# u and B loaded as 64 zero-padded rows on a new pitch in a Mamba scan on one core

## The reference

```
normed = rmsnorm(xn); x_z, z = split(normed @ in_proj_W)
xc = silu(conv4(x_z) + conv_b); dt = clip(softplus(xc @ dt_W + dt_b), 0.001, 0.1)
Bp = xc @ B_W; Cp = xc @ C_W; A = -exp(A_log)
for t in 0..511:
    h = exp(dt_t * A) * h + dt_t * B_t * x_t      # h is (8, 256, 64)
    y_t = sum_n h * C_t
x1 = xn + (y * silu(z)) @ out_proj_W; x1 + gated MLP(rmsnorm(x1)); + binary MLP(xn)
```

## Time and profile before

| | |
|---|---|
| runs | 1114.2, 1123.52, 1129.43 us |
| profiled execution, its own time | 1115.98 us |
| its span, first to last instruction | 1114.2 us |
| mean granted TensorE clock | 0.960 |
| PE, DVE, ACT, POOL busy | 87%, 84%, 82%, 76% of the span |
| HBM read, written | 303.24 MB, 22.02 MB |

### The profile page before, as it was taken

One profiled execution on the slowest core, in us unless ns is written; L12 is line 12 of the kernel. 1 busy time (PEld: TensorE's weight loads), 2 busy tenths in 40 slices (PEclk: granted clock), 3 DMA queues, 4 the chain that ended last, 5 costly groups with the idle time before them and its releaser, 6 DMA issues.

```text
span 1114.2 us, 27718 instructions
## 1 busy us (share of the span) xinstructions
PE 967.9 (87%) x8006; PEld 426.6 (38%) x8006; DVE 935.2 (84%) x2131; ACT 908.7 (82%) x1093; POOL 847.9 (76%) x1216
## 2 busy tenths in 40 slices
PE   5998883668999999998999887899998899999897
PEld 3555540113333343433333332334343334343436
DVE  5677663799989999997998887899998899999983
ACT  1666776789999999997988887899997899998980
POOL 6555513789888889887888786898887788988880
PEclk9999996789999999999999999899999899999999
DMA  4234358999999999997999999799999799999940
GB/s 139 81 136 180 136 200 298 345 327 355 351 343 334 345 355 350 345 344 268 356 341 332 319 328 318 271 351 352 353 349 333 280 366 343 339 356 340 335 148 10
DMA packets 76758, 327.39 MB, mean 294 GB/s; under 512 B 13472, under 2 KB 32800, under 8 KB 41504
## 3 DMA queue, kind: packets, MB, share of 16 engines
q1 hardware_dynamic: 76576, 325.30, 83.6%
HBM read 303.24 MB, written 22.02 MB: 292 GB/s over the span
## 4 chain that ended last, share of the span: by engine, by line
DVE 27%; PE 25%; POOL 19%; issue 16%; DMA 5%; ACT 5%; SPq 2%; DVEq 1%; POOLq 0%; ACTq 0%
POOL decayed L593 13%; DVE ps L1221 9%; PE ps L798 8%; DVE state L1232 7%; PE ps L743 5%; PE ps L897 5%; DMA decay<-dt_stage 4%; PE ps L883 3%; DVE h L1336 2%; ACT state L1030 2%; DVE h L1345 1%; DVE soft L1147 1%; POOL soft L543 1%; SPq L392 1%; POOL u_rest L553 1%
## 5 line engine op out<-in xcount | busy, mean ns | idle before, releaser
L593 POOL TENSOR_TENSOR decayed<-decay,state 128x256 f32<-128x256 f32 x1024 | 725.5, 733 | 169.1 <-DVE state L1232 125.4
L1010 ACT ACTIVATE decay<-decay,a_col 128x2048 f32<-128x2048 f32 x256 | 512.7, 2003 | 46.3 <-DMA decay<-dt_stage 36.5
L1232 DVE TENSOR_TENSOR state<-decayed,ps 128x256 f32<-128x256 f32 x1024 | 403.1, 417 | 55.4 <-POOL decayed L593 40.0
L1221 DVE TENSOR_TENSOR ps<-decay,ps 128x512 f32<-128x512 f32 x512 | 352.6, 689 | 40.5 <-ACT state L1030 17.2
L1030 ACT COPY state<-ps 128x512 f32<-128x512 f32 x512 | 288.9, 582 | 64.6 <-issue 43.2
L798 PE MATMUL ps<-state,c_cols 128*32 128x256 f32 x4096 | 338.2, 403 | 0.1
L743 PE MATMUL ps<-moving,b_rows 64*128 64x256 bf16 x1024 | 204.3, 281 | 100.5 <-DVE ps L1221 96.3
L750 PE MATMUL ps<-moving,b_rows 64*128 64x256 bf16 x1024 | 205.4, 282 | 12.0 <-DMA b_rows<-b_stage 12.0
L883 PE MATMUL ps<-h,w 128*128 128x256 f32 x512 | 175.8, 429 | 1.0 <-DVE h L1336 0.8
L743 PEld LDWEIGHTS ps<-moving,b_rows 64*128 64x128 bf16 x1024 | 58.4, 94 | 274.0 <-DVE ps L1221 172.3
L798 PEld LDWEIGHTS ps<-state,c_cols 128*32 128x32 f32 x4096 | 82.0, 109 | 113.4 <-issue 101.3
(11 more groups left out here) (124 smaller groups left out, 825.3 us busy)
## 6 DMA issues: line engine op xcount, KB each, us to landing
decay<-dt_stage SPq DMA_DIRECT2D x512, 512.0 KB, 6.6
moving<-u_stage SPq DMA_DIRECT2D x64, 288.0 KB
b_stage<-b_parts SPq DMA_DIRECT2D x24, 384.0 KB, 3.8
b_rows<-b_stage SPq DMA_DIRECT2D x64, 144.0 KB
dt_stage<-dt_tok SPq DMA_DIRECT2D x8, 512.0 KB, 3.1
u_stage<-u_parts SPq DMA_DIRECT2D x8, 512.0 KB, 2.8
x_tok<-in_L_attn_x_dram SPq DMA_DIRECT2D x4, 512.0 KB, 3.5
u_stage<-u_parts SPq DMA_DIRECT2D x8, 256.0 KB, 2.1
```

What stands on the lines that cost most here:

```text
L593: nc.gpsimd.tensor_tensor(decayed[:, p], decay[:, dec_slot(m, k), p, k % TS, :], state[:, (k - 1) % RING, p * E:(p + 1) * E], ALU.mult).th ...
L1010: nc.scalar.activation(pair, pair, ACT.Exp, scale=a_col[:, 2:3]).then_inc(decay_ready, 1)
L1221: nc.vector.tensor_tensor(ps[:, acc_bank(m, k), :].rearrange("p (q e) -> p q e", q=HQ), decay[:, dec_slot(m, k), HQ:Q, k % TS, :], ps[:, a ...
L1232: nc.vector.tensor_tensor(state[:, k % RING, p * E:(p + 1) * E], decayed[:, p], ps[:, SELFP + k % 2, p * E:(p + 1) * E], ALU.add).then_inc ...
```

## The change

- The 3 x 3 pairs of parts become 4 x 4 (NS = NP + 1): a fourth part of u and of B, and its pairs, are zeros. A load of u or B thus has 4 * 4 * 4 = 64 rows and they go to every second partition (`slice(hq, P, HQ)`), so that the two hq cover all 128 partitions of `moving`.
- The rows of the stages are T + TC = 528 tokens long instead of 512: 264 KB for u and 132 KB for B. `dt_stage` has one more row group of 8 KB for each bb.
- SP stores the zero parts at the beginning, 3 * B = 24 transfers (`store_pads`), from a corner of `moving` that POOL sets to zero first; SP waits for all of them before the first load of the scan.
- The two memsets of `moving` (L578 on POOL, L1202 on DVE) are gone.

```diff
+    TROW = T + TC
-    ROWS = NP * NP * HALF
-    RSTEP = 3
-    RFIRST = HROW + RSTEP - 1 - RSTEP * (ROWS // 2)
+    NS = NP + 1
+    ROWS = NS * NS * HALF
+    assert HQ * ROWS == P
...
-    u_stage = nc.dram_tensor("u_stage", (HQ, HQ, 2, NP, T, E), BF16, kind="Internal").ap()
-    dt_stage = nc.dram_tensor("dt_stage", (2, T // TS, Q, TS, E), F32, kind="Internal").ap()
-    b_stage = nc.dram_tensor("b_stage", (HQ, HQ, 2, NP, NP, T, 2 * N), BF16, kind="Internal").ap()
+    u_stage = nc.dram_tensor("u_stage", (HQ, HQ, 2, NS, TROW, E), BF16, kind="Internal").ap()
+    dt_stage = nc.dram_tensor("dt_stage", (2, T // TS + 1, Q, TS, E), F32, kind="Internal").ap()
+    b_stage = nc.dram_tensor("b_stage", (HQ, HQ, 2, NS, NS, TROW, 2 * N), BF16, kind="Internal").ap()
...
         def product_rows(hq):
-            first = RFIRST - 2 + hq
-            return slice(first, first + RSTEP * (ROWS - 1) + 1, RSTEP)
+            return slice(hq, P, HQ)
...
                          u_stage[hq, :, :, :, bass.ds(t, TC), :].rearrange("f b i t e -> (f b i) (t e)")
-                         .unsqueeze(1).broadcast_to([HALF * NP, NP, TC * E])
+                         .unsqueeze(1).broadcast_to([HALF * NS, NS, TC * E])
...
+                def store_pads(n):
+                    q, bb = n // 2, n % 2
+                    u_rows, b_planes = u_stage[q % HQ, q // HQ, bb], b_stage[q % HQ, q // HQ, bb]
+                    zeros = moving[:, 1, 0:2 * NS].rearrange("p t e -> p (t e)")
+                    sp.dma_start(u_rows[NP, 0:T].rearrange("(p j) e -> p (j e)", j=NJ),
+                                 zeros[:, 0:NJ * E]).then_inc(pads_stored, 16)
+                    sp.dma_start(b_planes[NP, :, 0:T].rearrange("k (p j) n -> p k (j n)", j=NJ),
+                                 zeros[:, 0:NS * NJ * 2 * N].rearrange("p (k n) -> p k n", k=NS)).then_inc(pads_stored, 16)
+                    sp.dma_start(b_planes[0:NP, NP, 0:T].rearrange("k (p j) n -> p k (j n)", j=NJ),
+                                 zeros[:, 0:NP * NJ * 2 * N].rearrange("p (k n) -> p k n", k=NP)).then_inc(pads_stored, 16)
...
+                sp.wait_ge(pad_zeroed, 1)
+                for n in range(B):
+                    store_pads(n)
                 for q in range(Q):
...
                 sp.wait_ge(rows_zeroed, 2)
+                sp.wait_ge(pads_stored, 16 * PADS)
...
                 nc.gpsimd.memset(zero_b[:], 0.0)
+                nc.gpsimd.memset(moving[:, 1, 0:2 * NS], 0.0).then_inc(pad_zeroed, 1)
...
-                    nc.gpsimd.memset(moving[:, 0], 0.0)
                     nc.gpsimd.memset(b_rows[:, 0], 0.0).then_inc(rows_zeroed, 1)
...
-                    nc.vector.memset(moving[:, 1], 0.0)
                     nc.vector.memset(b_rows[:, 1], 0.0).then_inc(rows_zeroed, 1)
```

More of the change, by code:

```diff
@@ L46, in mamba_and_binary_mlp_block @@
     HROW = P // 2
-    ROWS = NP * NP * HALF
-    RSTEP = 3
-    RFIRST = HROW + RSTEP - 1 - RSTEP * (ROWS // 2)
-    assert RFIRST > 0 and HROW + HQ - 1 + RSTEP * (ROWS // 2) <= P
+    NS = NP + 1
+    ROWS = NS * NS * HALF
+    assert HQ * ROWS == P
     QE = Q * E
@@ L118, in mamba_and_binary_mlp_block @@
         b_loaded = [sem("b_loaded0"), sem("b_loaded1")]
+        pad_zeroed = sem("pad_zeroed")
         rows_zeroed = sem("rows_zeroed")
+        pads_stored = sem("pads_stored")
         const_set = sem("const_set")
@@ L212, in mamba_and_binary_mlp_block @@
         STORES = 2 + NP
+        PADS = 3 * B
         def batches(eng, slot, filling=None):
@@ L400, in store @@
                     wait_all(sp, [(S["dt_ready"], n + 1)])
-                    sp.dma_start(dt_stage[bb, :, q].rearrange("(p c) s e -> p c (s e)", s=TS, p=P),
+                    sp.dma_start(dt_stage[bb, 0:T // TS, q].rearrange("(p c) s e -> p c (s e)", s=TS, p=P),
                                  dt_tok[:, bb].rearrange("p (c s) e -> p c (s e)", s=TS)
@@ L416, in store @@
                         wait_all(sp, [(S[ready], n + 1)])
-                        sp.dma_start(stage[i0:i1].rearrange("i (p j) e -> p i (j e)", j=NJ),
+                        sp.dma_start(stage[i0:i1, 0:T].rearrange("i (p j) e -> p i (j e)", j=NJ),
                                      parts[:, bb, i0:i1].rearrange("p i j e -> p i (j e)")
                                      ).then_inc(S[f"parts_stored{bb}"], 16)
+                sp.wait_ge(pad_zeroed, 1)
+                for n in range(B):
+                    store_pads(n)
                 for q in range(Q):
```

## The result

The changed kernel took 1180.29 us (median of four runs, 1177.52 to 1183.88) against 1120.83 us before in the same comparison. The ratio is 1.058, 95% interval 1.0534 to 1.0626: 5.8% slower. The forecast was 1112 us with a range up to 1170.

The account below looks back on a forecast made before the run. The compute chain was taken to bound a clean body at 54 us, DMA just under it. Span 1114.2 - 6 - 1 - 1 = 1106 us, 1108 us with 1.8 us around it; forecast median 1112 us, range 1090 to 1170 us.

Parts of the forecast that it names:

- The bound: Scan body: the compute chain sets a clean body at 54 us, with DMA just under the point where it takes over.
- Loss by slow packets: Scan loads of u and B: slow stretches cost 4.8 us of DMA per body, taken as removed by the change.
- The sum: Scan body if the loss grows with bytes: 50.1 + 8.5 = 58.6 us of DMA against 54 us compute, +74 us.
- The rival: Scan becomes DMA-bound: slow packets stay and grow with the 64 distinct rows, 1155 to 1190 us; chance 0.2.
- Memsets: Before the scan: DVE and POOL lose their memsets of `moving`; -1 us (0 to -2.1).
- Pads: Preparation: SP issues 24 pad stores in about 12 us, in a gap, done by some 53 us; cost 0.
- Start of the scan: First two chunks' loads: faster packets against more zeros, including PE's 12.3 us wait; together -1 us (-3 to +3).
- The rate with fast packets: Scan body afterwards: 403 GB/s as full rate, an ordinary body at 373 GB/s or so, still 54 us.

## Why the prediction was wrong, point by point

- **The bound** was read rightly. DMA stood just under the compute chain: the run with an eighth of u and B shows the floor at 1101 us, about 20 us below the kernel before in the same comparison. I had only 9.4 us for the loop from two long bodies of one execution, plus the start.
- **The failed step is "Loss by slow packets ... I take 'removed'".** I named three things that set load_u and load_b apart (pitch, destination rows, number of engines), saw that the change took all three away, and let the loss of 4.8 us per body go. Instead the bodies became 4.1 us longer on average. None of the three was the cause by itself: not the pitch (nothing clear of the noise in four pairs of runs), not the destination rows (the changed kernel has those of the dt loads and is slow), not the number of engines (48 rows are slow on 16). What I did not list is the form of the source against the destination. The load of u kept a source of two dimensions, 12 x 3 before and 16 x 4 afterwards, and it can be read in the diff: `.unsqueeze(1).broadcast_to(...)`. For B the change did what I expected, once u no longer slowed it: it is fast with u from one row and B untouched (1102 us, landing after 6.8 us). Against the changed kernel this cause is shown. That the kernel before was slow for its form as well (36 rows, u with one step or as 12 x 3) is shown only in so far as its data, addresses and partition step are ruled out.
- **The sum** with the loss growing was in the text: 58.6 us of DMA per body, +4.6 us over the chain, +74 us in all. Measured +4.1 us per body on average and +66.6 us on the span (the ordinary body shown, +7.2, is one of the long ones). The rival's 1155 to 1190 us held 1180. Its mechanism, many distinct rows, is refuted: 64 distinct rows are fast and 36 equal ones slow. Its arithmetic (the loss goes with the bytes of the slow loads, from a point at which the slack is used up) came out near, in part by luck: it leaves out what the bodies show beyond DMA times. A late dt load holds ACT, ACT holds the slots, and DMA then idles (the slices of 121 and 158 GB/s), and PE's granted clock falls behind such a wait; in other bodies the chain covers the loss.
- **What the Trainium skill said.** Page "DMA: Bandwidth & Descriptors", section "Latency and other measured facts": next to nothing lost at 512 KiB, and so nothing to win by padding 256 and 128 KB. That was my inference from the skill's figures, and the runs agree with it: 0.06 to 0.4% between the medians of the two pitches in the four pairs, no more than their intervals allow for. I had it in the rival to which I gave 0.2. The Trainium skill's rule for the number of engines (same page, section "Why a DMA increments its semaphore by 16 and not by 1") agrees with the completions in both traces. It does not follow that 16 are faster.
- **Memsets** -1 us: the scan begins 1.4 us earlier. That is the change's: the first load_u is at 173.3 to 174.7 us in the seven runs with the memsets and unchanged stores, at 171.6 to 173.2 us in the seven without. **Pads** 0: right in effect, though the issues took twice as long, 25.9 us instead of 12. One took SP up to 1.3 us, once 2.4, instead of 0.5, while DMA was busy throughout. The last is issued at 38.16 us, the load of x for n = 4 only behind it, at 39.02 us instead of the 25 that I had, and the store of n = 0 at 40.40 instead of 39.39 us, which nobody waited for. **Start of the scan**: PE's wait 13.5 us instead of 12.3, within the range given but on the other side of my -1 us.
- **The rate with fast packets** was right, though not of the changed kernel: with 64 single rows an ordinary body takes 54 us at some 375 GB/s and DMA is off the path.

## What to carry to other kernels

When a load makes its neighbours slow, list every respect in which it differs from a fast one, the dimensions of both access patterns included, and change them one at a time before paying bytes for all of them together. Zeros that round a transfer up are worth it only if they bring it into the fast form; here 78% more bytes of u and B cost nothing with 64 rows against 64 (0.4 to 0.5% below the kernel before) and 5.8% without. Read the rate in short slices against the best slice, since the busy share is at 9 tenths either way.

## What the runs showed of the hardware that I had not expected

- A load from DRAM of 64 rows to every second partition runs at full rate beside others when its source is 64 rows with one step, or one row 64 times. A source of 16 x 4 for the same 64 rows, 48 rows against 48 on 16 engines, and 36 rows on 12 engines do not: dt loads land in 6.6 to 9.3 us (median) instead of 5.9 to 6.1, and the rate falls to between 200 and 290 GB/s instead of some 400 for microseconds.
- As far as tried, this does not depend on the addresses: equal or different rows in either form, 128 and 256 against 132 and 264 KB apart in either, contiguous in the slow one. Not tried: other numbers of rows from partition 0 on, or 64 rows elsewhere.
- Why this is so is open. The Trainium skill, page "DMA: Bandwidth & Descriptors", section "The descriptor swizzle", has it that in a transfer to 128 partitions each engine writes the partitions of one SBUF port; if something like it held for 64 rows against 64 and not for the other forms, engines would meet at the ports. That is my guess. The trace names neither engine nor partition of a packet, so no run here shows it.
- SP's time for one issue of load_u depends on its form, but does not tell fast from slow. The medians are 0.47 us for 64 rows with one step (fast), 0.56 for 48 with one step, 0.59 for 16 x 4, 0.78 for 36 with one step and 0.84 for 12 x 3 (all slow).
